# Rotary attention: row maxima of short key spans taken for two or four heads in one instruction, in 38 pieces over 19 of 20 steps

## The chip, the cores and the metric

One core of one Trainium2 chip runs the whole layer in one launch. The metric is the device time of that launch in microseconds, median of several runs.

## The reference

A layer of four residual parts on x of 1024 tokens and 512 channels. Only the first is touched:

```python
x = x + attn_a(layernorm(x))     # rotary, 32 heads of 16: the part changed
x = x + ffn(layernorm(x)); x = x + attn_b(layernorm(x)); x = x + ffn(layernorm(x))
# attn_a, causal, T = 1024:
scores = einsum('bqhd,bkhd->bhqk', rot(xq), rot(xk)) * 16 ** -0.5   # masked where k > q
out = einsum('bhqk,bkhd->bqhd', softmax(scores), xv).reshape(B, T, C) @ wo.T
```

## The kernel before

Rotary attention works on 8 groups of GA = 4 heads. To keep the softmax exact, the maximum of every row of scores must be known before the exponentials. So each group is scored twice. The first scoring, with queries on the partitions, exists only for the maxima: TensorE (PE) writes a *piece*, a 128-query tile against up to 512 keys, into one bank of PSUM (L940, and a causal mask added by a second matmul, L943, where the piece touches the diagonal), and VectorE (DVE) reduces it to one number per row (L1041). A group has 48 pieces, for each head 8 query tiles, of 128, 256, 384 or 512 keys, tiles 4 to 7 with a second span. The maxima of the 4 x 8 units are then split into three bf16 parts (`split_max`, five short DVE instructions in a chain, L552 to L561), turned by PE (`turn_max`, L949), copied out (L1046) and stored by three DMAs as three extra rows of the queries. The second scoring (L968, mask L972) contracts over 99 rows, so that the maximum comes off in the matmul itself; ScalarE (ACT) takes the exponential of two banks at once (L1028, L1030); PE multiplies by the values (`mix`, L986, fp32, four heads in strips of 32 columns).

The order is written by hand. Each group has 20 steps. In step `tau`, PE does the second scoring of one set of heads, then the `mix` blocks that are due, then the pieces of the *next* group that `a_pieces_before` gives to step t' = (tau + 6) mod 20 (A_SHIFT = 6), and, where due, `turn_max` and the turning of the output rows (L995). DVE follows the same list: maxima of the pieces, `split_max` at t' = SPLIT_AT, copy of the turned maxima at t' = MAX_AT. `a_pieces_before` deals the pieces out in equal shares of width + 128 over the first A_LAST_PIECE steps t'. Below, "step n" is step n of the group that is being exponentiated, so t' = 0 is step 14, t' = 17, 18, 19 are steps 11, 12, 13. `mix` blocks fall into steps 0, 1, 5, 6, 7, 11, 12, 15, 16 and 19; the output rows are turned in steps 2 and 8.

The pieces have three banks (4, 5, 7): PE must wait for the maximum of the piece three before. The engines are in order, so a PE wait for a bank also holds the next scoring, and with it ACT. The second scoring of a step waits for the exponential of two steps before.

`FirstMaxima` does the pieces of group 0, with six banks, between the projections of the values (L499, L502, reduce L538), and then as many pieces of group 1 as t' = 0 to 5 hold (`score_next`, L515, L518, reduce L546), before the loop of the 8 groups starts. After the loop comes `stream_block`, everything from the output projection of this attention on.

Of the kernel before, what the change touches and what calls it, by code (L numbers as in the profile page):

```python
# [11 lines left out]
ALU = mybir.AluOpType  # L12
ACT = mybir.ActivationFunctionType
AX = mybir.AxisListType

P = 128
T = 1024
C = 512
NT = T // P
KC = C // P  # L20
W = 512
# [3 lines left out]
GA = 4  # L25
# [15 lines left out]
def key_spans(i):  # L41

    w = P * (i + 1)
    return [(0, min(w, W))] + ([(W, w)] if w > W else [])
# [370 lines left out]
A_ROWS = 6 * DA  # L415
A_UNITS = GA * NT
A_LINKS = 5
A_TERMS = ((0, 0), (0, 1), (0, 2), (1, 0), (1, 1), (2, 0))
A_PIECES = [(hh, i, c, span) for hh in range(GA) for i in range(NT) for c, span in enumerate(key_spans(i))]
A_FIRST = sorted(A_PIECES, key=lambda piece: piece[1])  # L420
A_LAST_PIECE = 17
A_SHIFT = 6
A_PIECE_BANKS = (4, 5, 7)


def a_pieces_before(t):

    total = sum(k1 - k0 + W // 4 for _, _, _, (k0, k1) in A_PIECES)
    n, width = 0, 0
    while n < len(A_PIECES) and width * A_LAST_PIECE < t * total:  # L430
        width += A_PIECES[n][3][1] - A_PIECES[n][3][0] + W // 4
        n += 1
    return n


class FirstMaxima:
# [52 lines left out]
    def score_pieces(self, pe, h):  # L489
        pe.wait_ge(self.made, 2)  # L490
        pe.wait_ge(self.rows_in[h], 16 * 2 * len(A_TERMS))
        for n, (hh, i, c, (k0, k1)) in enumerate(A_FIRST):
            if i // 2 != h:
                continue
            if n >= len(self.BANKS):
                pe.wait_ge(self.credited["piece_max"], 1 + n + 1 - len(self.BANKS))
            out = self.ps[:, self.BANKS[n % len(self.BANKS)], 0:k1 - k0]
            last_span = k1 == P * (i + 1)
            last = pe.matmul(out, self.q_st[0][0:A_ROWS, hh, i * P:(i + 1) * P], self.k_st[0][0:A_ROWS, hh, k0:k1],  # L499
                             start=True, stop=not last_span)  # L500
            if last_span:
                last = pe.matmul(out[:, k1 - k0 - P:k1 - k0], self.const["ident_bf"][:, :], self.mask[:, :],  # L502
                                 start=False, stop=True)
            last.then_inc(self.credited["piece_scored"], 1)

    def score_next(self, pe, first, end):

        for n in range(first, end):
            hh, i, c, (k0, k1) = A_PIECES[n]
            if n == 0:  # L510
                pe.wait_ge(self.loaded[1], 16 * 2 * len(A_TERMS))
            pe.wait_ge(self.credited["piece_max"], 1 + len(A_PIECES) + n + 1 - len(A_PIECE_BANKS))
            out = self.ps[:, A_PIECE_BANKS[n % len(A_PIECE_BANKS)], 0:k1 - k0]
            last_span = k1 == P * (i + 1)
            last = pe.matmul(out, self.q_st[1][0:A_ROWS, hh, i * P:(i + 1) * P], self.k_st[1][0:A_ROWS, hh, k0:k1],  # L515
                             start=True, stop=not last_span)
            if last_span:
                last = pe.matmul(out[:, k1 - k0 - P:k1 - k0], self.const["ident_bf"][:, :], self.mask[:, :],  # L518
                                 start=False, stop=True)
            last.then_inc(self.credited["piece_scored"], 1)  # L520

    def turn_max(self, pe):
# [9 lines left out]
        dve.wait_ge(self.made, 2)  # L532

    def max_of_pieces(self, dve):
        for n, (hh, i, c, (k0, k1)) in enumerate(A_FIRST):
            u = hh * NT + i
            dve.wait_ge(self.credited["piece_scored"], 1 + n + 1)
            dve.tensor_reduce(self.part_max[:, c, u:u + 1], self.ps[:, self.BANKS[n % len(self.BANKS)], 0:k1 - k0],  # L538
                              AX.X, ALU.max).then_inc(self.credited["piece_max"], 1)

    def max_of_next(self, dve, first, end):
        for n in range(first, end):
            hh, i, c, (k0, k1) = A_PIECES[n]
            u = hh * NT + i
            dve.wait_ge(self.credited["piece_scored"], 1 + len(A_PIECES) + n + 1)
            dve.tensor_reduce(self.part_max[:, c, u:u + 1], self.ps[:, A_PIECE_BANKS[n % len(A_PIECE_BANKS)], 0:k1 - k0],  # L546
                              AX.X, ALU.max).then_inc(self.credited["piece_max"], 1)

    def split_max(self, dve, start=1, pieces_done=None):
        link = self.credited["link"]  # L550
        dve.wait_ge(self.credited["piece_max"], 1 + len(A_FIRST) if pieces_done is None else pieces_done)
        dve.tensor_tensor(self.row_max[:, :], self.part_max[:, 0, :], self.part_max[:, 1, :], ALU.max).then_inc(link, 1)  # L552
        dve.wait_ge(link, start + 1)
        dve.tensor_scalar(self.max_part[:, 0, :], self.row_max[:, :], -1.0, None, ALU.mult).then_inc(link, 1)
        dve.wait_ge(link, start + 2)
        dve.scalar_tensor_tensor(self.max_rest[:, :], self.row_max[:, :], -1.0, self.max_part[:, 0, :],
                                 ALU.mult, ALU.subtract).then_inc(link, 1)
        dve.wait_ge(link, start + 3)
        dve.tensor_copy(self.max_part[:, 1, :], self.max_rest[:, :]).then_inc(link, 1)
        dve.wait_ge(link, start + 4)  # L560
        dve.tensor_tensor(self.max_part[:, 2, :], self.max_rest[:, :], self.max_part[:, 1, :],  # L561
                          ALU.subtract).then_inc(link, 1)
# [7 lines left out]
def rotary_projection_block(nc, ctx, norm, weights, xt_h, xt_l, w_h, w_l, v_all, o_all, spare, stage_room, first, const, ps, parts_dram, x_in):  # L570
# [4 lines left out]
    with ExitStack() as own:  # L575
# [65 lines left out]
        def _(pe):  # L641
# [53 lines left out]
            first.score_next(pe, 0, 2)  # L695
            first.turn_max(pe)
            first.score_next(pe, 2, a_pieces_before(A_SHIFT))

        @block.scalar
# [42 lines left out]
        def _(dve):  # L742
# [32 lines left out]
            first.max_of_next(dve, 0, 2)  # L775
            first.take_max(dve)
            first.max_of_next(dve, 2, a_pieces_before(A_SHIFT))


# [14 lines left out]
def rotary_attention_block(nc, ctx, v_all, o_all, spare, wo_h, wo_l, first, const, ps, parts_dram, wo_dram, raw_room, later_loads):  # L794
# [9 lines left out]
    def sem(name):  # L804
        return credited[name] if name in credited else ctx.enter_context(nc.semaphore(f"ra_{name}"))
# [3 lines left out]
    UNITS = A_UNITS  # L809
    PIECES = A_PIECES  # L810
    NP = len(PIECES)
    SPLIT_AT, MAX_AT = 17, 18
    ROWS = A_ROWS + A_PARTS
    LINKS = A_LINKS
    PIECE_BANKS = A_PIECE_BANKS
    SHIFT = A_SHIFT
    with ExitStack() as own:
        def sb(name, shape, dt=F32):
            return own.enter_context(nc.sbuf_tensor(f"ra_{name}", shape, dt))

        q_st = first.q_st + [sb(f"q_st{b}", [P, GA, T], BF16) for b in range(2, A_BUFS)]
        k_st = first.k_st + [sb(f"k_st{b}", [P, GA, T], BF16) for b in range(2, A_BUFS)]
        v4 = [sb(f"v4{b}", [P, NT, GA, 32]) for b in range(2)]
        pt = [sb("pt0", [P, GA, 2 * W]), sb("pt1", [P, GA, 2 * W]), spare.rearrange("p (h n) -> p h n", h=GA)]
        mask, part_max, max_part, max_rows = first.mask, first.part_max, first.max_part, first.max_rows
# [9 lines left out]
        piece_max = sem("piece_max")  # L835
# [15 lines left out]
        def loads_of(g):  # L851

            return g // A_BUFS + 1 - (1 if g % A_BUFS == 0 else 0)

        def count(each, g, n):
            return 1 + each * g + n
# [70 lines left out]
        @block.tensor  # L927
        def _(pe):
            def piece(g, n):

                hh, i, c, (k0, k1) = PIECES[n]
                b = g % A_BUFS
                if n == 0:
                    pe.wait_ge(loaded[b], 16 * 12 * loads_of(g))
                pe.wait_ge(piece_max, count(NP, g, n + 1 - len(PIECE_BANKS)))
                if n == 0:
                    pe.wait_ge(max_out, count(1, g, 0))
                out = ps[:, PIECE_BANKS[n % len(PIECE_BANKS)], 0:k1 - k0]
                last_span = k1 == P * (i + 1)
                last = pe.matmul(out, q_st[b][0:A_ROWS, hh, i * P:(i + 1) * P], k_st[b][0:A_ROWS, hh, k0:k1],  # L940
                                 start=True, stop=not last_span)
                if last_span:
                    last = pe.matmul(out[:, k1 - k0 - P:k1 - k0], const["ident_bf"][:, :], mask[:, :],  # L943
                                     start=False, stop=True)
                last.then_inc(piece_scored, 1)

            def turn_max(g):
# [51 lines left out]
            for tau in range(NGA * S + 3):  # L999
# [3 lines left out]
                for gg in range(NGA):  # L1003
                    for k in range(SETS):
                        n = tau - (S * gg + A_SET_END[k] + 2)
# [29 lines left out]
        @block.vector  # L1035
        def _(dve):
            def max_of_piece(g, n):
                hh, i, c, (k0, k1) = PIECES[n]
                u = hh * NT + i
                dve.wait_ge(piece_scored, count(NP, g, n + 1))  # L1040
                dve.tensor_reduce(part_max[:, c, u:u + 1], ps[:, PIECE_BANKS[n % len(PIECE_BANKS)], 0:k1 - k0], AX.X, ALU.max).then_inc(piece_max, 1)  # L1041

            def take_max(g):
                dve.wait_ge(max_turned, count(1, g, 1))
# [1007 lines left out]
```

## Time and profile before

| | us |
|---|---|
| runs | 1602.8, 1601.39, 1602.74; median 1602.74 |
| profiled execution | 1604.81, span of its instructions 1603.0 |
| rotary attention loop in it | 140.3 to about 404 |
| TensorE busy | 1507.2 (94%) |
| VectorE busy | 1111.8 (69%) |
| ScalarE busy | 796.5 (50%) |
| mean granted TensorE clock | 0.984 |

Busy time counts an instruction from its start to its last result; on PE and DVE the next one starts before that, so shares of busy time overstate how full an engine is. The granted clock is 1.00 at 2.4 GHz and 0.50 at 1.2 GHz.

### The profile page before, as it was taken

What the parts mean: (1) busy time and instruction counts of PE and PEld (TensorE: products, weight loads), DVE (VectorE), ACT (ScalarE), POOL (GpSimd) and SP (SyncE); (2) the same over time, 40 slices, a digit from 0 to 9 for tenths busy, and PEclk for the clock granted to TensorE, in tenths of its full rate; (3) what the DMA queues carried; (4) which work ended last, traced back from release to release, by engine and by line L of the source; (5) the groups of instructions that cost most, each with busy time, mean ns of one, the idle gap of its engine ahead of it and who ended that gap; (6) DMA issues with size and microseconds to landing.
All of it is one profiled execution on the core that took longest, in us unless ns stands there. A gap on an engine that the chain in (4) does not pass through costs nothing.

```text
span 1603.0 us, 25452 instructions
## 1 busy us (share of the span) xinstructions
PE 1507.2 (94%) x8968; PEld 1174.6 (73%) x8968; DVE 1111.8 (69%) x2866; ACT 796.5 (50%) x2087; POOL 440.3 (27%) x435
## 2 busy tenths in 40 slices
PE   3998999998897899999999999999999999999997
PEld 2863444443686788888888888888888888888776
DVE  5658777771575577687678677678767767767873
ACT  3522555557333355555555555555554555555441
POOL 4102000010452341341332234144134143224332
PEclk9997999999999899999999999999999999999999
DMA  4363344301100100100100010010010010000000
GB/s 150 96 140 56 41 61 59 43 2 54 54 21 1 40 27 1 40 21 8 40 14 14 1 40 27 1 40 27 1 40 27 1 40 14 14 19 22 7 21 27
DMA packets 40206, 54.27 MB, mean 34 GB/s; under 512 B 5776, under 2 KB 21392, under 8 KB 40080
## 3 DMA queue, kind: packets, MB, share of 16 engines
q1 hardware_dynamic: 40080, 52.65, 13.8%
q8 instruction: 72, 1.18, 0.3%
q14 instruction: 54, 0.44, 0.1%
HBM read 44.04 MB, written 8.39 MB: 33 GB/s over the span
## 4 chain that ended last, share of the span: by engine, by line
PE 65%; DVE 3%; issue 2%; POOL 2%; ACT 2%; POOLq 0%; ACTq 0%; DVEq 0%
PE ps L50 18%; PE ps L52 18%; PE ps L51 18%; PE ps L1528 7%; PE ps L1503 2%; DVE ab_qt_l L1777 1%; POOL ab_o_l L1424 1%; PE ps L241 1%; PE ps L1505 0%; ACT ab_o_raw L1695 0%; POOL wo L1392 0%; ACT ab_kt_h L1674 0%; POOL ab_o_h L1422 0%; DVE ab_pt_l L1785 0%; ACT ab_squares L1665 0%
## 5 line engine op out<-in xcount | busy, mean ns | idle before, releaser
L1653 ACT ACTIVATE prob<-prob,ab_neg_max 128x128 f32<-128x128 f32 (+7 forms) x256 | 200.7, 784 | 241.7 <-DVE ab_neg_max L1768 240.6
L1785 DVE TENSOR_TENSOR ab_pt_l<-ps,ab_pt_h 128x512 fp32r<-128x512 f32 x288 | 198.0, 688 | 67.3 <-ACT ab_pt_h L1681 65.0
L1681 ACT CAST ab_pt_h<-ps 128x512 fp32r<-128x512 f32 x288 | 171.7, 596 | 127.2 <-PE ps L1528 126.6
L1768 DVE CUSTOM_DVE_ANT_0 prob<-ps,rel 128x512 f32<-128x512 f32 (+3 forms) x256 | 146.1, 571 | 102.6 <-PE ps L52 101.8
L50 PE MATMUL ps<-ab_w_h,ab_xt_h 128*128 128x512 f32 (+1 forms) x512 | 185.6, 362 | 5.0 <-DVE ab_v_l L1805 5.0
L1041 DVE TENSOR_REDUCE ra_part_max<-ps 128x1 f32<-128x512 f32 (+3 forms) x318 | 156.4, 552 | 48.3 <-PE ps L943 29.2
L1528 PE MATMUL ps<-ident,prob 128*128 128x128 f32 x1152 | 173.4, 273 | 4.6 <-DVE ab_qt_l L1777 3.3
L52 PE MATMUL ps<-ab_w_h,ab_xt_l 128*128 128x512 f32 (+1 forms) x512 | 174.4, 341 | 0.0
L51 PE MATMUL ps<-ab_w_l,ab_xt_h 128*128 128x512 f32 (+1 forms) x512 | 173.7, 339 | 0.0
L1793 DVE TENSOR_SCALAR prob<-prob,ab_recip 128x128 f32<-128x128 f32 (+7 forms) x256 | 164.1, 641 | 9.1
L1413 POOL TENSOR_TENSOR ab_rms<-ab_ms_eps,neg_half 128x5 f32<-128x5 f32 x64 | 76.3, 1192 | 318.0 <-DVE ab_ms_eps L1810 317.2
L1528 PEld LDWEIGHTS ps<-ident,prob 128*128 128x128 f32 x1152 | 138.1, 140 | 24.8 <-DVE ab_qt_l L1777 4.3
L1030 ACT ACTIVATE ra_pt<-ps 128x1024 f32<-128x1024 f32 x96 | 97.3, 1024 | 84.9 <-PE ps L972 72.7
L50 PE MATMUL ps<-ab_kt_h,ab_qt_h 128*128 128x512 f32 (+2 forms) x384 | 132.8, 346 | 0.2 <-DVE ab_neg_max L1768 0.2
L52 PE MATMUL ps<-ab_kt_h,ab_qt_l 128*128 128x512 f32 (+2 forms) x384 | 132.1, 344 | 0.0
L51 PE MATMUL ps<-ab_kt_l,ab_qt_h 128*128 128x512 f32 (+2 forms) x384 | 131.8, 343 | 0.0
L50 PE MATMUL ps<-ab_pt_h,ab_v_h 128*128 128x512 f32 x288 | 127.2, 442 | 2.5 <-ACT ab_o_raw L1695 2.3
L1422 POOL CAST ab_o_h<-ab_o_raw 128x512 fp32r<-128x512 f32 x64 | 42.0, 657 | 289.0 <-ACT ab_o_raw L1695 257.1
L51 PE MATMUL ps<-ab_pt_l,ab_v_h 128*128 128x512 f32 x288 | 113.6, 394 | 0.0
L52 PE MATMUL ps<-ab_pt_h,ab_v_l 128*128 128x512 f32 x288 | 113.6, 394 | 0.0
L50 PEld LDWEIGHTS ps<-ab_w_h,ab_xt_h 128*128 128x128 f32 x512 | 97.8, 191 | 19.6 <-DVE ab_v_l L1805 5.9
L51 PEld LDWEIGHTS ps<-ab_w_l,ab_xt_h 128*128 128x128 f32 x512 | 98.0, 191 | 14.1
(232 smaller groups left out, 3487.9 us busy)
## 6 DMA issues: line engine op xcount, KB each, us to landing
f_raw<-in_wqkv SPq DMA_DIRECT2D x32, 384.0 KB, 3.7
f_raw<-in_wbo SPq DMA_DIRECT2D x32, 256.0 KB, 2.6
ra_first_rows<-parts SPq DMA_DIRECT2D x36, 128.0 KB, 6.7
parts<-pa_stage SPq DMA_DIRECT2D x12, 256.0 KB, 3.1
parts<-f_raw SPq DMA_DIRECT2D x12, 256.0 KB, 3.3
ra_q_st<-parts SPq DMA_DIRECT2D x24, 128.0 KB, 6.5
ra_k_st<-parts SPq DMA_DIRECT2D x24, 128.0 KB, 6.8
f_raw<-in_wf SPq DMA_DIRECT2D x8, 324.0 KB, 3.3
```

Source lines behind the costliest of these rows:

```text
L50: pe.matmul(out, lh, rh, start=start, stop=False)
L51: pe.matmul(out, lh, rl, start=False, stop=False)
L52: return pe.matmul(out, ll, rh, start=False, stop=stop)
L1030: act.activation(pt[k % 3][:, h, :], pair.rearrange("p a b -> p (a b)"), ACT.Exp).then_inc(exped, 1)
L1041: dve.tensor_reduce(part_max[:, c, u:u + 1], ps[:, PIECE_BANKS[n % len(PIECE_BANKS)], 0:k1 - k0], AX.X, ALU.max).then_inc(piece_max, 1)
L1413: pool.tensor_tensor(rms[:, t % 2, :], ms_eps[:, t % 2, :], const["neg_half"][:, 0:GB + 1], ALU.pow).then_inc(rms_ready, 1)
L1528: last = pe.transpose(ring_bank("p", u, j)[:, h * P:(h + 1) * P], prob[:, u % 2, h, j * P:(j + 1) * P], const["ident"][:, :])
L1653: act.activation(prob[:, t % 2, h, 0:w], prob[:, t % 2, h, 0:w], ACT.Exp, bias=neg_max[:, t % 2, h, pieces_per_head(t % NT) - 1:pieces_per ...
L1681: act.copy(pt_h[:, n % PT, :], ring_bank("p", u, j)).then_inc(pt_high, 1)
L1768: dve.tensor_tensor_reduce(out=prob[:, t % 2, h, k0:k1], in0=ps[:, n % 2, a:b], in1=const["rel"][:, SLIDE - i * P + k0:SLIDE - i * P + k1] ...
L1785: dve.tensor_tensor(pt_l[:, n % PT, :], ring_bank("p", u, j), pt_h[:, n % PT, :].bitcast(F32), ALU.subtract).then_inc(emptied, 1)
L1793: dve.tensor_scalar(prob[:, t % 2, h, 0:w], prob[:, t % 2, h, 0:w], recip[:, t % 2, h:h + 1], None, ALU.mult).then_inc(normed, 1)
```

## The change

Spans of 128 keys are scored for four heads and spans of 256 for two heads into one bank, one head behind the other, and one `tensor_reduce` with a three-dimensional operand takes the maxima of all of them. Spans of 384 and 512 keys stay as they are. A group has 38 pieces in place of 48, ordered by query tile instead of by head, in the loop as well. Every matmul stays. A_LAST_PIECE goes from 17 to 19, SPLIT_AT from 17 to 18 and MAX_AT from 18 to 19. The diff, cut to its core (the three places that score and the three that reduce all call the new functions):

```diff
-A_PIECES = [(hh, i, c, span) for hh in range(GA) for i in range(NT) for c, span in enumerate(key_spans(i))]
-A_FIRST = sorted(A_PIECES, key=lambda piece: piece[1])
-A_LAST_PIECE = 17
+def a_pieces():
+    pieces = []
+    for i in range(NT):
+        for c, (k0, k1) in enumerate(key_spans(i)):
+            heads = min(GA, W // (k1 - k0))
+            pieces += [(hh, heads, i, c, (k0, k1)) for hh in range(0, GA, heads)]
+    return pieces
+A_PIECES = a_pieces()
+A_LAST_PIECE = 19
 def a_pieces_before(t):
-    total = sum(k1 - k0 + W // 4 for _, _, _, (k0, k1) in A_PIECES)
+    total = sum(heads * (k1 - k0) + W // 4 for _, heads, _, _, (k0, k1) in A_PIECES)
     n, width = 0, 0
     while n < len(A_PIECES) and width * A_LAST_PIECE < t * total:
-        width += A_PIECES[n][3][1] - A_PIECES[n][3][0] + W // 4
+        _, heads, _, _, (k0, k1) = A_PIECES[n]
+        width += heads * (k1 - k0) + W // 4
         n += 1
     return n
+def score_piece_a(pe, piece, bank, q_rows, k_rows, ident, mask):
+    first, heads, i, _, (k0, k1) = piece
+    for hh in range(first, first + heads):
+        out = bank[:, (hh - first) * (k1 - k0):(hh - first + 1) * (k1 - k0)]
+        last_span = k1 == P * (i + 1)
+        last = pe.matmul(out, q_rows[0:A_ROWS, hh, i * P:(i + 1) * P], k_rows[0:A_ROWS, hh, k0:k1],
+                         start=True, stop=not last_span)
+        if last_span:
+            last = pe.matmul(out[:, k1 - k0 - P:k1 - k0], ident[:, :], mask[:, :], start=False, stop=True)
+    return last
+def max_of_piece_a(dve, part_max, piece, bank):
+    first, heads, i, c, (k0, k1) = piece
+    maxima = part_max[:, c, :].rearrange("p (h i) -> p h i", i=NT)
+    return dve.tensor_reduce(maxima[:, first:first + heads, i],
+                             bank[:, 0:heads * (k1 - k0)].rearrange("p (h k) -> p h k", h=heads), AX.X, ALU.max)
...
-    SPLIT_AT, MAX_AT = 17, 18
+    SPLIT_AT, MAX_AT = 18, 19
```

## Rows read from the trace of the kernel before

**Rows 1.** The page, part 1 (busy us) and the granted clock of part 2.
```profile
PE 1507.2 (94%) x8968; PEld 1174.6 (73%) x8968; DVE 1111.8 (69%) x2866; ACT 796.5 (50%) x2087; POOL 440.3 (27%) x435
...
PEclk9997999999999899999999999999999999999999
```
**Rows 2.** Busy time by stretch (windows): group 3, and group 7, which has no pieces.
```profile
243.70:277.70 34.00, 32.36 (x270) 14.82 (x273) 25.81 (x59) 19.51 (x22) 0.61 (x1) 1.00 0.38 47
...
376.70:400.00 23.30, 20.23 (x175) 7.89 (x178) 1.36 (x4) 18.45 (x21) 1.27 (x1) 1.00 0.21 69
```
**Rows 3.** The turning of the maxima, source view of L949: first and last start.
```profile
L949 PE MATMUL ps<-ident_bf,ra_max_part x7: 257/257/257, 163.3 to 367.4; 128*96 128x128 bf16 x7
```
**Rows 4.** Groups by form, 0 to 330 us, two forms of L1041; then timeline, DVE.
```profile
L1041 DVE TENSOR_REDUCE ra_part_max<-ps 128x1 f32<-128x512 f32 x134 | 89.2, 684 | 25.8 <-PE ps L940 16.3 <-PE ps L943 9.5
...
L1041 DVE TENSOR_REDUCE ra_part_max<-ps 128x1 f32<-128x128 f32 x44 | 12.4, 282 | 4.7 <-PE ps L943 4.7
...
257.84 2.55 DVE L1041 TENSOR_REDUCE ra_part_max<-ps 128x1 f32<-128x384 f32 x5 [0.61 <-PE ps L943]
```
**Rows 5.** Timeline, PE matmuls, steps 6 to 8 of group 3: start, duration.
```profile
255.93 0.27 PE L940 MATMUL ps<-ra_first_rows 96*128 96x256 bf16 x1
256.04 0.22 PE L943 MATMUL ps<-ra_mask,ident_bf 128*128 128x128 bf16 x1
256.10 0.59 PE L968 MATMUL ps<-ra_q_st,ra_k_st 99*128 99x512 bf16 x2
256.62 0.86 PE L986 MATMUL ps<-ra_pt,ra_v 128*32 128x128 f32 x16
257.41 0.34 PE L940 MATMUL ps<-ra_first_rows 96*128 96x384 bf16 x1
...
258.14 0.60 PE L968 MATMUL ps<-ra_q_st,ra_k_st 99*128 99x512 bf16 x2
258.57 0.22 PE L940 MATMUL ps<-ra_first_rows 96*128 96x128 bf16 x1
```
**Rows 6.** Waits in group 3, 243.7 to 277.7: total us, times, longest.
```profile
PEld ps L940 <- DVE ra_part_max L1041: 10.0, 20, 0.8
...
DVE ra_part_max L1041 <- PE ps L943: 4.4, 7, 1.2
```
**Rows 7.** Timeline, ACT: step 2 to 3 of group 3, and of group 7.
```profile
247.80 1.02 ACT L1030 ACTIVATE ra_pt<-ps 128x1024 f32<-128x1024 f32 x1 [0.45 <-PE ps L972]
250.31 1.02 ACT L1030 ACTIVATE ra_pt<-ps 128x1024 f32<-128x1024 f32 x1 [1.49 <-PE ps L972]
...
379.77 1.02 ACT L1030 ACTIVATE ra_pt<-ps 128x1024 f32<-128x1024 f32 x1
381.12 1.02 ACT L1030 ACTIVATE ra_pt<-ps 128x1024 f32<-128x1024 f32 x1 [0.33 <-PE ps L972]
```
**Rows 8.** Timeline around the turning of the maxima in group 2.
```profile
229.63 0.19 DVE L552 TENSOR_TENSOR ra_row_max<-ra_part_max 128x32 f32<-128x32 f32 x1
...
230.52 0.19 DVE L561 TENSOR_TENSOR ra_max_part<-ra_max_rest,ra_max_part 128x32 bf16<-128x32 f32 x1
...
231.34 0.12 PEld L949 LDWEIGHTS ps<-ident_bf,ra_max_part 128*96 128x96 bf16 x1 [0.84 <-DVE ra_max_part L561]
```
**Rows 9.** Timeline ahead of the loop, DVE and PE.
```profile
110.31 6.99 DVE L538 TENSOR_REDUCE ra_part_max<-ps 128x1 f32<-128x512 f32 x16 [3.25 <-PE ps L499]
...
137.78 2.02 DVE L546 TENSOR_REDUCE ra_part_max<-ps 128x1 f32<-128x384 f32 x4 [0.17 <-PE ps L518]
...
114.72 0.48 PE L50 MATMUL ps<-a_w_h,wo 128*128 128x512 f32 x1
...
131.06 0.34 PE L524 MATMUL ps<-ident_bf,ra_max_part 128*96 128x128 bf16 x1 [1.21 <-DVE ra_max_part L561]
```
**Rows 10.** Windows of PE at a low share, with the granted clock.
```profile
84.00:88.00 4.00, 1.43 (x11) 1.13 (x10) 2.37 (x6) 2.61 (x7) 0.00 (x0) 1.00 0.88 269
88.00:92.00 4.00, 4.00 (x13) 3.12 (x12) 1.78 (x3) 1.14 (x2) 0.00 (x0) 0.57 0.17 49
...
1500.00:1505.00 5.00, 3.31 (x26) 2.96 (x24) 3.64 (x9) 2.98 (x8) 0.00 (x0) 1.00 0.00 0
```

More of the change, by code:

```diff
@@ L491, in score_pieces @@
         pe.wait_ge(self.rows_in[h], 16 * 2 * len(A_TERMS))
-        for n, (hh, i, c, (k0, k1)) in enumerate(A_FIRST):
-            if i // 2 != h:
+        for n, piece in enumerate(A_PIECES):
+            if piece[2] // 2 != h:
                 continue
@@ L496, in score_pieces @@
                 pe.wait_ge(self.credited["piece_max"], 1 + n + 1 - len(self.BANKS))
[L497 to L503, printed above, removed]
+            last = score_piece_a(pe, piece, self.ps[:, self.BANKS[n % len(self.BANKS)], :], self.q_st[0], self.k_st[0],
+                                 self.const["ident_bf"], self.mask)
             last.then_inc(self.credited["piece_scored"], 1)
@@ L508, in score_next @@
         for n in range(first, end):
-            hh, i, c, (k0, k1) = A_PIECES[n]
             if n == 0:
@@ L512, in score_next @@
             pe.wait_ge(self.credited["piece_max"], 1 + len(A_PIECES) + n + 1 - len(A_PIECE_BANKS))
[L513 to L519, printed above, removed]
+            last = score_piece_a(pe, A_PIECES[n], self.ps[:, A_PIECE_BANKS[n % len(A_PIECE_BANKS)], :], self.q_st[1],
+                                 self.k_st[1], self.const["ident_bf"], self.mask)
             last.then_inc(self.credited["piece_scored"], 1)
@@ L534, in max_of_pieces @@
     def max_of_pieces(self, dve):
-        for n, (hh, i, c, (k0, k1)) in enumerate(A_FIRST):
-            u = hh * NT + i
+        for n, piece in enumerate(A_PIECES):
             dve.wait_ge(self.credited["piece_scored"], 1 + n + 1)
-            dve.tensor_reduce(self.part_max[:, c, u:u + 1], self.ps[:, self.BANKS[n % len(self.BANKS)], 0:k1 - k0],
-                              AX.X, ALU.max).then_inc(self.credited["piece_max"], 1)
+            max_of_piece_a(dve, self.part_max, piece, self.ps[:, self.BANKS[n % len(self.BANKS)], :]
+                           ).then_inc(self.credited["piece_max"], 1)
     def max_of_next(self, dve, first, end):
         for n in range(first, end):
-            hh, i, c, (k0, k1) = A_PIECES[n]
-            u = hh * NT + i
             dve.wait_ge(self.credited["piece_scored"], 1 + len(A_PIECES) + n + 1)
-            dve.tensor_reduce(self.part_max[:, c, u:u + 1], self.ps[:, A_PIECE_BANKS[n % len(A_PIECE_BANKS)], 0:k1 - k0],
-                              AX.X, ALU.max).then_inc(self.credited["piece_max"], 1)
+            max_of_piece_a(dve, self.part_max, A_PIECES[n], self.ps[:, A_PIECE_BANKS[n % len(A_PIECE_BANKS)], :]
+                           ).then_inc(self.credited["piece_max"], 1)
     def split_max(self, dve, start=1, pieces_done=None):
         link = self.credited["link"]
-        dve.wait_ge(self.credited["piece_max"], 1 + len(A_FIRST) if pieces_done is None else pieces_done)
+        dve.wait_ge(self.credited["piece_max"], 1 + len(A_PIECES) if pieces_done is None else pieces_done)
         dve.tensor_tensor(self.row_max[:, :], self.part_max[:, 0, :], self.part_max[:, 1, :], ALU.max).then_inc(link, 1)
@@ L929, in piece @@
             def piece(g, n):
-                hh, i, c, (k0, k1) = PIECES[n]
                 b = g % A_BUFS
@@ L937, in piece @@
                     pe.wait_ge(max_out, count(1, g, 0))
[L938 to L944, printed above, removed]
+                last = score_piece_a(pe, PIECES[n], ps[:, PIECE_BANKS[n % len(PIECE_BANKS)], :], q_st[b], k_st[b],
+                                     const["ident_bf"], mask)
                 last.then_inc(piece_scored, 1)
@@ L1037, in max_of_piece @@
             def max_of_piece(g, n):
-                hh, i, c, (k0, k1) = PIECES[n]
-                u = hh * NT + i
                 dve.wait_ge(piece_scored, count(NP, g, n + 1))
-                dve.tensor_reduce(part_max[:, c, u:u + 1], ps[:, PIECE_BANKS[n % len(PIECE_BANKS)], 0:k1 - k0], AX.X, ALU.max).then_inc(piece_max, 1)
+                max_of_piece_a(dve, part_max, PIECES[n], ps[:, PIECE_BANKS[n % len(PIECE_BANKS)], :]).then_inc(piece_max, 1)
             def take_max(g):
```

## The prediction

> **What bounds the kernel now.** I read the page first: PE is busy 94% of the span at almost full clock, DVE 69% [rows 1]. That is an average over stages, so I cut out the stage that changes. The maxima are turned once per group, 7 times between 163.3 and 367.4, so a group takes (367.4 - 163.3) / 6 = 34.0 us [rows 3]. In a group PE is busy 32.4 us, DVE 25.8, ACT 19.5 [rows 2]. These figures count instructions that overlap, so what an engine really needs must come from start to start.
>
> PE [rows 5]: a matmul of 256 columns 0.11 us (255.93 to 256.04), one of 128 0.06, two of 512 0.43 (258.14 to 258.57), so 0.215 each and 0.16 for 384; `mix` blocks of 256 and 128 columns together 0.79 (256.62 to 257.41), about 1.05 for 512. Each of the two scorings has 8 matmuls of 128, 8 of 256, 8 of 384, 24 of 512 and 32 masks: 0.48 + 0.88 + 1.28 + 5.16 + 1.92 = 9.7 us. The `mix` has 4608 columns, 9 x 1.05 = 9.5 us. With about 1 us for turning rows and maxima: 19.4 + 9.5 + 1 = 29.9 us. The group takes 34.0, so PE stands still for about **4.1 us** of it.
>
> DVE [rows 4]: a reduce of 512 shows 684 ns, one of 128 shows 282. But five in a row (384, 512, 512, 128, 512, whose durations add to 2.88 with 0.555 for 384 between its neighbours) take 2.55 us, so each next one starts 0.083 before the end of the last. Start to start it is 0.60 for 512, 0.465 for 384, 0.33 for 256, 0.20 for 128: 0.13 per 128 columns and about 0.065 per instruction. The 48 reduces need 8 x (0.20 + 0.33 + 0.465) + 24 x 0.60 = 22.4 us, all DVE work about 25 of 34. DVE isn't the bound on average.
>
> What the two do to each other is the loss. The view of waits shows PE's weight loads of pieces waiting for DVE 20 times, 10.0 us (part of it under matmuls still running), and DVE waiting for PE 7 times, 4.4 us, in the same group [rows 6]. The two alternate, because three banks hold only three pieces. In step 2, where four pieces fall, ACT's rhythm is 2.51 us against 1.35 in group 7 without pieces [rows 7]. The four pieces and their masks need 0.79 on PE; the other 0.4 is waiting.
>
> **The change, part by part.** *Matmuls*: none is removed; PE's 29.9 us stay. *Reduces*: 8 of 128 become 2 of 4 x 128, 8 of 256 become 4 of 2 x 256. At the price of a plain 512 they take 6 x 0.60 against 8 x 0.20 + 8 x 0.33, 3.6 against 4.25: DVE saves **0.65 us** per group. The trace has no reduce of several rows. Bounds: the cost of one plain 512 (0.60) from below; from above four separate 128s (0.80) and two 256s (0.66), 0.65 dearer per group in all, which is the old cost. I take 0.60, since start to start goes with the columns. DVE has slack, so of this nothing counts directly; the rest is in how the pieces fall.
>
> The Trainium skill ("VectorE: DVE Perf Modes", "The DRAIN you can't avoid") says that the next DVE instruction doesn't start until the pipe is empty, so each reduce would hold DVE for all of its shown duration. By that the ten instructions fewer would save 10 x 0.148 = 1.5 us per group. The trace doesn't agree: 2.88 us of durations fit in 2.55.
>
> *Spreading*: 48 pieces in 17 steps put 2 to 4 pieces, 0.8 to 1.6 us of DVE, into a step; the dearest bursts lie in steps without `mix` (2, 4, 10, 14, 17, 18), where PE itself needs only 1.0 to 1.2 us, so it runs into the banks. 38 in 19 put 1 to 3, nearly always 2 (1.2 us), into a step. I carried three clocks (PE, DVE, ACT) through the 20 steps with the durations above and ACT's 1.02 (0.60 for the short sets), once for each dealing, every instruction starting when its engine is free and what it waits for is done. Waits for a bank, before: steps 2, 4, 8, 10, 14, 18 with 0.7, 0.7, 0.4, 0.6, 0.2, 0.9, and 0.1 elsewhere, **3.6 us**. After: steps 8, 10, 18 with 0.2, 0.6, 0.1, **0.9 us**, and 0.1 for an exponential. The walk over the old pieces gives a group of 33.1 us, 0.9 short of the 34.0 measured, so I trust its difference more than its level.
>
> *SPLIT and MAX one step later*: this is a wait that is added. Before, the last pieces fall in step 10, `split_max` follows in step 11, and PE asks for it in step 12, after two scorings and two `mix` blocks of 512, over 2.5 us of other work. The chain L552 to L561 takes 230.52 + 0.19 - 229.63 = 1.08 us, and was done at 230.71 while PE came to L949 at 231.34: no wait [rows 8]; the 0.84 shown there is under a running `mix`. After, the last piece is in step 12 and `turn_max` in step 13, which has no `mix`: between them PE has one scoring, 0.43 to 0.54 us. DVE needs the last pieces (0.6 to 1.0 us with latency), then the chain 1.1, then about 0.1. PE waits 0.6 + 0.6 + 1.1 + 0.1 - 0.5, in the walk **1.7 us**, in every one of the 7 groups. Queued behind it on PE is the scoring of step 14, for which ACT then waits; on DVE the copy of the turned maxima. Bounds: 1.2 if DVE is level with PE, 2.9 if it is two pieces behind. Nothing covers it. The stores of the maxima are then issued a step later but still 6 steps, some 10 us, ahead of their use in step 0, and the queue of SP has nothing behind them for the next 3 us; I cost them at nothing. The first piece of the next group waits for the copy of the turned maxima (0.4 us), under the scoring of step 14.
>
> Per group: 3.6 - 0.9 - 0.1 - 1.7 = **0.9 us**, 6 times; the last group with pieces gets only steps 0 to 13 of it, 0.6. Loop: 6 x 0.93 + 0.6 = 6.2 us.
>
> *Ahead of the loop*: DVE sets the pace there. In the stretch of tiles 4 and 5, 16 reduces take 6.99 us, and PE is let on to the projections at 114.72 [rows 9], when the tenth of 16 is reduced (110.31 + 5 x 0.60 + 4 x 0.20 + 0.33 = 114.4). With 11 pieces it is the fifth: 110.31 + 5 x 0.60 + 0.1 = 113.4, and PE is through 0.34 later, at 113.8: 0.9 us earlier, and all behind it too. The tail, from the turning at 131.06 to the end of the last reduce, 137.78 + 2.02 = 139.80 [rows 9], holds 18 reduces, 9.5 us by duration and 8.0 start to start; with 13 (9 x 0.60 + 4 x 0.465) it holds 7.3, and with the waits for PE that it has now the gain is 0.6 to 0.9 us. Together **1.8 us**. Clock is low there (slices 3 and 4 of the row [rows 1]), but DVE leads.
>
> *After the loop* nothing changes, and its start waits for the end of the loop, not for a load.
>
> Sum: 6.2 + 1.8 = 8.0 us. The profiled execution, 1604.81, would be 1596.8; it lies 2.07 above the median, so the median goes to 1602.74 - 8.0 = **1594.7 us**.
>
> **Rivals.** (a) *The new wait takes the gain.* If DVE comes to step 12 two pieces behind, PE waits 2.9 us, not 1.7, and the group gains 3.5 - 0.9 - 2.9 = -0.3 to 0; what is left is the 1.8 us ahead of the loop: 1600.9. Against: steps 11 and 12 have a `mix` of 512 each, in which DVE catches up. For: they now hold pieces, which before they didn't.
>
> (b) *More is gained.* If the banks hardly ever fill, the 0.9 that I leave goes too, and the wait at the turning is 1.2: 0.9 + 0.9 + 0.5 = 2.3 per group, but part of it meets ACT's 1.02 per step in the light steps; with 1.6 per group, 6.6 x 1.6 + 1.8 = 12.4: 1590.3.
>
> (c) *Slower: the clock.* A stand of 1.7 us in each group might let the granted clock fall. After a stretch with PE busy 1.43 of 4 us it fell, to a mean of 0.57 over the next 4 [rows 10]; at 1.2 GHz for 3.4 us (0.43 x 4 / 0.5) PE loses half of them, 1.7 us. Seven times is 12 us, more than the 8.0: 1606.7. It decides as soon as it happens in 5 of 7 groups. Against: 1500 to 1505 has PE busy 3.31 of 5, the same 1.7 us standing, and the clock stays at 1.00. The Trainium skill has the rule ("TensorE: Matmul & The Clock Gate", "HAM oscillation — how this bites in real kernels"): idling between bursts of matmuls brings the clock down and costs more than the idling. By it alone this rival would be the likelier one; the row of 1500 speaks against it at this size.
>
> (d) *Merged reduces cost as their parts.* Then DVE loses its 0.65 us; a third of it at most comes through at full banks: 1.5 us less gain, 1596.2. This is inside the forecast's range.
>
> **How the numbers follow.** Forecast 0.66, with (d) in it, spread 1591.5 to 1598; (b) 0.15, (a) 0.13, (c) 0.06. The range for 8 in 10 goes from 1590 to 1600.9, into (b) and up to (a). A measurement of this kernel tells about 0.2%, 3.2 us, from no change, so faster is the forecast and (b), 0.81; same is (a), 0.13; slower is (c), 0.06.
>
> **What would show it.** Right: period of L949 about 33.1 us; PE's waits for L1041 fewer than half; a wait of PE for L561 of 1.5 to 2 us uncovered, once per group; reduces of 4 x 128 at about 684 ns; the loop's first scoring at about 138.5 instead of 140.3; the clock 1.00 from 146 to the end of the loop. Wrong: a period of 34 with the wait at L561 near 3 us is (a), a clock of 0.50 behind the turnings is (c), a period below 32.5 is (b). If the period stays and the wait is as forecast, the walk's account of the bank waits was wrong.

## The result, and the profile after

The changed kernel takes 1592.18 us (median of 4 runs, 1591.04 to 1593.13) against 1602.77 (1601.39 to 1602.94): ratio 0.9936, 95% interval 0.9918 to 0.9953, faster by 10.6 us. Forecast were 1594.7 in 1590 to 1600.9. The profiled execution took 1592.62. One of the four runs of the kernel over 17 steps, below, took 2144.83 us at a mean granted clock of 0.655 and is left out of its median.

The page of the changed kernel, busy time and granted clock, answers [rows 1]:

```profile
PE 1493.7 (94%) x8968; PEld 1170.9 (74%) x8968; DVE 1106.1 (70%) x2786; ACT 795.9 (50%) x2087; POOL 440.7 (28%) x435
...
PEclk9997999999999999999999999999999999999999
```

PE has the same 8968 matmuls, DVE 80 instructions fewer (8 groups of ten). The shares are the same as before; they don't tell that anything has happened. Where the time went is read from the places that can be matched in both traces. First the turning of the maxima (L960 now, L949 in [rows 3]), in the source view:

```profile
L960 PE MATMUL ps<-ident_bf,ra_max_part x7: 257/257/257, 160.3 to 359.1; 128*96 128x128 bf16 x7
```

(359.1 - 160.3) / 6 = **33.13 us** per group, against 34.0. Then the first exponential of group 0 and of group 7, timeline of ACT, before and after:

```profile
141.63 1.02 ACT L1030 ACTIVATE ra_pt<-ps 128x1024 f32<-128x1024 f32 x1 [20.50 <-PE ps L972]
...
376.76 1.02 ACT L1030 ACTIVATE ra_pt<-ps 128x1024 f32<-128x1024 f32 x1 [1.12 <-PE ps L972]
```

```profile
139.03 1.02 ACT L1041 ACTIVATE ra_pt<-ps 128x1024 f32<-128x1024 f32 x1 [19.09 <-PE ps L983]
...
367.44 1.02 ACT L1041 ACTIVATE ra_pt<-ps 128x1024 f32<-128x1024 f32 x1 [1.12 <-PE ps L983]
```

| part of the span | before | after | difference |
|---|---|---|---|
| ahead of the loop, to the first exponential | 141.6 | 139.0 | -2.6 |
| groups 0 to 6 | 235.1 | 228.4 | -6.7 |
| group 7 and all behind it | 1226.2 | 1223.1 | -3.1 |
| span | 1603.0 | 1590.5 | -12.5 |

The last part of the span, with 3.1 us of difference, has no changed instruction in it. Windows of the 200 us from the start of group 7, before and after (the columns are as in [rows 2]; the third from the end is the granted clock):

```profile
376.80:576.80 200.00, 175.93 (x1021) 137.94 (x1015) 110.24 (x323) 84.15 (x229) 68.17 (x85) 0.94 0.10 31
```

```profile
367.50:567.50 200.00, 174.60 (x1036) 137.20 (x1029) 111.54 (x327) 85.38 (x232) 71.60 (x89) 0.97 0.10 31
```

The clock is 0.94 before and 0.97 after: some 12 us less at 1.2 GHz fit in (0.03 x 200 / 0.5), and 15 matmuls more have started. Over the whole part the clock record has 26.5 us at 1.2 GHz before and 15.3 after. The twelve kernels of this case don't differ here, and in their traces the two go together: from 15 us at 1.2 GHz and 1223.1 us for this part to 26.5 us and 1226.3 us. So these 3.1 us are put down to the clock, not to the change.

Below, a *stand* is time in which PE could run nothing. The new one, in the timeline of group 3 (start, duration, idle before in brackets):

```profile
257.36 0.39 PE L454 MATMUL ps<-ra_first_rows 96*128 96x512 bf16 x1
...
257.65 0.59 PE L979 MATMUL ps<-ra_q_st,ra_k_st 99*128 99x512 bf16 x2
257.85 0.69 DVE L464 TENSOR_REDUCE ra_part_max<-ps 128x1 f32<-128x512 f32 x1 [0.80 <-PE ps L457]
...
258.57 0.19 DVE L570 TENSOR_TENSOR ra_row_max<-ra_part_max 128x32 f32<-128x32 f32 x1
...
259.46 0.19 DVE L579 TENSOR_TENSOR ra_max_part<-ra_max_rest,ra_max_part 128x32 bf16<-128x32 f32 x1
259.70 0.26 PE L960 MATMUL ps<-ident_bf,ra_max_part 128*96 128x128 bf16 x1 [1.46 <-DVE ra_max_part L579]
...
260.61 1.02 ACT L1041 ACTIVATE ra_pt<-ps 128x1024 f32<-128x1024 f32 x1 [1.31 <-PE ps L983]
```

The last piece of the group is issued at 257.36. DVE waits 0.80 for it, so it has no older piece left to do. It reduces this one and runs its chain. PE, which had one scoring to do, stands 1.46 us with nothing running, and ACT then waits 1.31 for the next scoring. In [rows 8] the same wait was drawn as 0.84 under a running `mix` and cost nothing. And waits of PE between 140 and 400, before and after:

```profile
PE ps L940 <- DVE ra_part_max L1041: 9.9, 40, 0.5
```

```profile
PE ps L960 <- DVE ra_max_part L579: 10.2, 7, 1.5
...
PE ps L454 <- DVE ra_part_max L464: 2.8, 7, 0.4
```

The 9.9 us in 40 waits for the reduces are now 2.8 in 7, but 10.2 for the chain come in. Taken as they are, these rows say that PE waits *more* than before, although the loop is shorter. The view begins a wait only at the modelled end of the matmul in front, and so leaves part of each stand out. An example from before, in step 2 of group 3:

```profile
248.30 0.22 PE L943 MATMUL ps<-ra_mask,ident_bf 128*128 128x128 bf16 x1
248.82 0.34 PE L940 MATMUL ps<-ra_first_rows 96*128 96x384 bf16 x1 [0.30 <-DVE ra_part_max L1041]
```

From start to start these are 0.52 us, the mask takes 0.06 of them, and 0.46 are a stand; the bracket says 0.30. Counted in this way for one group with the clock at 1.00 (what a start lies behind the one before it, less that matmul's columns at 2.4 GHz, stretches of over 0.03 us, the starts of and behind `mix` blocks left out; the last four kernels are experiments, below):

| kernel | period, us | stands at the banks | stand before the turning | period less all stands |
|---|---|---|---|---|
| before | 34.0 | 3.3 | 0 | 30.7 |
| changed | 33.1 | 0.8 | 1.6 | 30.7 |
| merged, 17 steps | 32.4 | 1.7 | 0 | 30.7 |
| merged, 18 steps | 32.5 | 1.4 | 0.4 | 30.7 |
| order alone, 17 steps | 33.4 | 2.7 | 0 | 30.7 |
| spreading alone (group with the clock at 1.00) | 35.5 | 2.8 | 1.9 | 30.7 |

The last column is the same for all within 0.1, so these two kinds of stand are the whole difference between the kernels' periods. The change takes away 2.5 us per group at the banks and adds 1.6 before the turning. The merged reduces cost what a plain one costs (groups by form, 0 to 330):

```profile
L464 DVE TENSOR_REDUCE ra_part_max<-ps 128x1 f32<-128x512 f32 x168 | 106.6, 684 | 27.4 <-PE ps L454 18.8 <-PE ps L457 8.1
...
L464 DVE TENSOR_REDUCE ra_part_max<-ps 128x2 f32<-128x512 f32 x30 | 19.9, 685 | 6.6 <-PE ps L457 6.6
L464 DVE TENSOR_REDUCE ra_part_max<-ps 128x4 f32<-128x512 f32 x15 | 10.4, 692 | 11.2 <-PE ps L457 11.2
```

### The profile page after: what moved, and what is told of

The parts are those of the page before. It is cut to its first block, busy times and chain, and to the rows that moved or that the text cites. A ratio compares the mean times of both kernels' runs of the same rounds, so it can differ in the third digit from the quotient of the medians.

```text
span 1590.5 us, 25372 instructions
## 1 busy us (share of the span) xinstructions
PE 1493.7 (94%) x8968; PEld 1170.9 (74%) x8968; DVE 1106.1 (70%) x2786; ACT 795.9 (50%) x2087; POOL 440.7 (28%) x435
## 4 chain that ended last, share of the span: by engine, by line
PE 65%; DVE 3%; issue 2%; POOL 2%; ACT 2%; POOLq 0%; ACTq 0%; DVEq 0%
PE ps L50 18%; PE ps L52 18%; PE ps L51 18%; PE ps L1537 7%; PE ps L1512 2%; DVE ab_qt_l L1786 1%; POOL ab_o_l L1433 1%; PE ps L241 1%; PE ps L1514 0%; ACT ab_o_raw L1704 0%; POOL wo L1401 0%; ACT ab_kt_h L1683 0%; POOL ab_o_h L1431 0%; DVE ab_pt_l L1794 0%; ACT ab_squares L1674 0%
## 5 line engine op out<-in xcount | busy, mean ns | idle before, releaser
L464 DVE TENSOR_REDUCE ra_part_max<-ps 128x1 f32<-128x512 f32 (+3 forms) x304 | 182.2, 656 | 62.0 <-PE ps L457 40.7
L1041 ACT ACTIVATE ra_pt<-ps 128x1024 f32<-128x1024 f32 x96 | 97.9, 1024 | 91.0 <-PE ps L983 74.1
```

The costliest lines, as they stand in the source:

```text
L464: return dve.tensor_reduce(maxima[:, first:first + heads, i], bank[:, 0:heads * (k1 - k0)].rearrange("p (h k) -> p h k", h=heads), AX.X, A ...
L1041: act.activation(pt[k % 3][:, h, :], pair.rearrange("p a b -> p (a b)"), ACT.Exp).then_inc(exped, 1)
```

## The experiments

Theory A is the prediction's: time was lost where DVE fills the three banks; the change takes most of that away and pays for the later turning. The change does three things at once (merging, a new order, 19 steps for 17), so the first four runs take them apart. The measure is the *period*, the time from one turning of the maxima to the next, taken from the first and the last of the seven. It repeats within 0.02 us from group to group as long as the clock stays the same, and doesn't see the clock behind the loop.

**Merged pieces over 17 steps, split and turning where they were.**

```diff
-A_LAST_PIECE = 19
+A_LAST_PIECE = 17
-    SPLIT_AT, MAX_AT = 18, 19
+    SPLIT_AT, MAX_AT = 17, 18
```

> Merged pieces, but dealt over 17 steps with the split and the turning where they were before the change (17, 18). Theory A (the gain comes from full banks that don't fill any more, and the later turning costs a wait of 1.5 us per group): the wait of PE before the turning goes, some bank waits come back; period of a group 33.14 - 0.8 = 32.3 us, total about 1587, faster than the changed kernel by some 5 us. Rival B (the gain is the spreading over 19 steps): most of the gain goes, period near 34, total above 1598.

```profile
L960 PE MATMUL ps<-ident_bf,ra_max_part x7: 257/257/257, 159.4 to 353.6; 128*96 128x128 bf16 x7
```

Period (353.6 - 159.4) / 6 = 32.37 us, forecast 32.3; 1589.8 us (three runs), ratio to before 0.9912 (0.9892 to 0.9932), forecast 1587. Rival B falls: the step from 17 to 19 doesn't bring the gain, it costs 0.77 us per group. PE's waits show the trade:

```profile
PE ps L454 <- DVE ra_part_max L464: 5.6, 14, 0.5
```

PE's waits for banks double from 2.8 to 5.6 us in the loop, and the 10.2 for the chain are gone from the view. From start to start it is the same: 0.9 us more per group at the banks, 1.6 less before the turning.

**Merged over 18 steps.** A_LAST_PIECE = 18, the rest as in the changed kernel.

> As the changed kernel, but the pieces are dealt over 18 steps; split and turning stay at 18 and 19. Theory A: the last pieces are done a step before the turning, PE waits for it 0.4 to 0.6 us instead of 1.5; bank waits up by 0.5; period 33.14 - 0.55 = 32.6 us, total about 1588.5. Rival B: between the changed kernel and the one over 17, that is a little slower than the changed one.

Period (352.6 - 157.6) / 6 = 32.50 us, forecast 32.6; 1588.46 us, ratio 0.9907 (0.989 to 0.9923). One step between the last piece and the turning is enough to bring the wait down: the view has 1.7 us in 7 waits in all. The total is below the one over 17 steps although the period is longer. In the profiled executions that is the stretch ahead of the loop, which this one left 2.7 us earlier, at a clock of 0.76 between 120 and 140 against 0.65. The two totals can't be told apart.

**The spreading alone**: the kernel before with A_LAST_PIECE = 19 and SPLIT_AT, MAX_AT = 18, 19.

> The kernel before with its 48 pieces in their old order, dealt over 19 steps, split and turning at 18 and 19. Theory A: bank waits hardly fall (one piece per bank is still a short reduce followed by long ones), the wait before the turning comes, about 2 us; period 34.0 + 1.4 = 35.4 us, total about 1612, slower than before. Rival B: most of the change's gain, period 33 to 33.5, total about 1596.

1619.49 us, ratio 1.0097 (1.008 to 1.0114): 16 us *slower* than before, and 7 more than A had said. The waits have the form that A gave, here of PE between 140 and 400:

```profile
PE ps L949 <- DVE ra_max_part L561: 12.5, 7, 1.8
PE ps L940 <- DVE ra_part_max L1041: 9.2, 27, 0.6
```

But the period, (385.7 - 165.5) / 6 = 36.7 by the source view, is 1.3 above the forecast. The turnings lie 35.46 us apart once, behind the one of group 3, and 36.9 to 37.0 us the other five times. Windows behind a turning, in group 2 (turned at 239.32) and in group 3 (at 276.35):

```profile
241.00:244.40 3.40, 3.40 (x17) 0.92 (x16) 1.02 (x2) 1.27 (x2) 0.00 (x0) 0.51 0.50 96
278.00:281.40 3.40, 3.40 (x33) 1.37 (x31) 1.94 (x4) 1.83 (x3) 0.00 (x0) 1.00 0.19 51
```

After the stand that ends at 239 the granted clock is 0.51 for 3.4 us, and the window has 17 matmuls; after the equal one that ends at 276 it stays 1.00, and the window has 33. So in this kernel the prediction's rival (c) happened, five times, at 1.4 to 1.6 us each (it had said 1.7). Where it didn't, A's period holds, 35.46 against 35.4. A's reason holds too: by the table above the stands at the banks fall only from 3.3 to 2.8.

**The order alone**: no merging, but pieces by query tile; 17 steps.

```diff
-            heads = min(GA, W // (k1 - k0))
+            heads = 1
```

> 48 pieces, none merged, but ordered by query tile instead of by head; 17 steps, split 17, turning 18. Tells the merging from the new order, both of which the change makes. Theory A: the order alone gives part, by the three clocks 0.6 us per group (period 33.4), total about 1598. Rival C (what counts is ten reduces and ten waits fewer): nothing, period 34.0.

1599.35 us (10 runs), ratio 0.9976 (0.9966 to 0.9985); period (363.0 - 162.7) / 6 = 33.38, forecast 33.4. It has ten reduces per group more than the changed kernel, and yet it gains 0.6 us per group on the kernel before. By head, short and long pieces alternate; by tile, like stands with like, and the steps get other bursts. Step 2 holds two pieces in place of four, and its stand goes from 0.66 us to none; step 18 goes from 0.88 to 0.43; the other steps together have 0.5 more. Why this order suits the steps better than another wasn't tested. Rival C falls as the whole story. Merging on top of it (32.37) gives another 1.0.

**Does the number of reduces count?** The changed kernel, banks shared, but one reduce for each head.

```diff
-    return dve.tensor_reduce(maxima[:, first:first + heads, i],
-                             bank[:, 0:heads * (k1 - k0)].rearrange("p (h k) -> p h k", h=heads), AX.X, ALU.max)
+    n = k1 - k0
+    for hh in range(heads):
+        u = (first + hh) * NT + i
+        last = dve.tensor_reduce(part_max[:, c, u:u + 1], bank[:, hh * n:(hh + 1) * n], AX.X, ALU.max)
+    return last
```

> The changed kernel, pieces still share banks, but the maxima of a bank are taken by one reduce for each head (four of 128, two of 256), 10 reduces more in a group. Theory A: DVE gives back its 0.65 us, of which 0.1 to 0.2 comes through at full banks: period 33.3 us. Rival (fewer DVE instructions are the gain): period 33.8 or more.

Period (359.2 - 159.7) / 6 = 33.25, 0.11 longer; 1594.89 us in one run. Ten DVE instructions fewer per group are worth 0.1 us of period. So of the 1.0 that merging brings, 0.9 must come from the banks: one bank carries four heads, or two, ten handovers between PE and DVE fewer per group, and with them another dealing of the pieces to the steps. These last two weren't taken apart.

**Is the wait before the turning on the path in full?** The last link of the chain is done again, two and four times more.

```diff
-A_LINKS = 5
+A_LINKS = 7
...
+        for extra in range(2):
+            dve.wait_ge(link, start + 5 + extra)
+            dve.tensor_tensor(self.max_part[:, 2, :], self.max_rest[:, :], self.max_part[:, 1, :],
+                              ALU.subtract).then_inc(link, 1)
```

> The changed kernel with the last instruction of the chain that splits the maxima done three times (7 links, not 5; same result), so that PE waits 0.44 us longer before the turning, 1.9 to 2.0 us. Theory A: the wait lies on the path in full: period 33.14 + 0.44 = 33.6 us. Theory C (the clock falls when PE stands for about 1.8 us in a group, as in the kernel with the spreading alone, where it was low for 20 us of the loop): some groups a further 1.5 us longer, at a granted clock of 0.5 for 3.4 us each.

> As before with 9 links, 0.88 us more, PE stands 2.4 us before the turning. Theory A: period 34.0 us, loop 6 us longer than in the changed kernel. Theory C: the clock falls in most groups, period 35.5, loop 14 to 16 us longer.

The waits of PE before the turning, in the kernel with two links more, and with four:

```profile
PE ps L964 <- DVE ra_max_part L583: 13.4, 7, 1.9
```

```profile
PE ps L964 <- DVE ra_max_part L583: 16.5, 7, 2.4
```

With two more, three of the six periods last 33.59 or 33.60 (0.45 longer, A) and three 35.19 or 35.20. The one run took 1603.06 us, and the kernel before, run beside it, 1603.52: nearly all of the gain is gone. With four more, all six periods are 34.05, (368.1 - 163.8) / 6, 0.91 longer, A again. The clock keeps its 1.00 behind the first six stands, though they are longer, and falls once, at the last turning, for 6.9 us at 0.51. The one run took 1606.53 us, and its loop is 10.4 us longer than in the changed kernel, not 6: 4.5 of it in groups 1 to 5, the rest in group 0, which begins with 5 us at half clock against 2.6, and in group 6 with its fall. So the wait counts in full, and theory C is half right: a stand of 1.8 to 1.9 us *can* be followed by a fall of the clock, a longer one needn't. Windows with two links more, behind the turning of group 0 (at 161.13) and of group 2 (at 231.52):

```profile
162.30:165.70 3.40, 3.40 (x21) 1.38 (x18) 1.33 (x2) 1.78 (x2) 0.00 (x0) 0.50 0.29 73
232.70:236.10 3.40, 3.40 (x34) 1.89 (x32) 2.09 (x4) 1.78 (x2) 0.00 (x0) 1.00 0.31 72
```

The stand in front is 1.9 us both times, so its length alone doesn't decide; what does is left open. In the changed kernel, with 1.5 us, the clock fell in no group.

**Ahead of the loop**: the changed kernel with the 48 single pieces for group 0 (`FirstMaxima` alone; the counts of the loop are shifted by ten).

> The changed kernel in the loop, but the 48 unmerged pieces for the first group, ahead of the loop. Theory A: the projections behind tiles 4 and 5 start 0.9 us later relative to the start of their pieces, period as in the changed kernel (33.14), the loop starts 0.9 to 1.2 us later than in the changed kernel. Rival (the 2.6 us that the start of the loop came earlier are the clock's): no difference beyond where the clock is low.

The stretch of tiles 4 and 5, the DVE timeline of the changed kernel, and then of this one:

```profile
110.08 6.68 DVE L464 TENSOR_REDUCE ra_part_max<-ps 128x1 f32<-128x512 f32 x11 [3.25 <-PE ps L454]
...
119.59 9.13 DVE L464 TENSOR_REDUCE ra_part_max<-ps 128x1 f32<-128x512 f32 x16 [2.83 <-PE ps L454]
```

```profile
110.71 6.99 DVE L467 TENSOR_REDUCE ra_part_max<-ps 128x1 f32<-128x512 f32 x16 [3.25 <-PE ps L457]
...
121.19 9.13 DVE L467 TENSOR_REDUCE ra_part_max<-ps 128x1 f32<-128x512 f32 x16 [3.48 <-PE ps L457]
```

From the first burst to the next are 9.51 us with merged pieces and 10.48 with single ones (10.47 in the kernel before), 0.97 apart, at a clock of 1.00 in both. The period is (360.5 - 161.6) / 6 = 33.15; one run, 1594.61 us. That the loop starts 1.04 later (first exponential at 140.07 against 139.03) looks like the same number, but two things cancel in it: this execution came to the stretch 0.63 later (110.71 against 110.08), and behind the last reduce ahead of the loop, where its clock was back at 1.00 and the other's at 0.50, it was 0.55 faster. So 1.0 of the 2.6 us is settled by the burst alone. 0.2 was there already when the stretch began (110.08 against 110.31 in [rows 9]); the other 1.4 is the tail with 13 pieces in place of 18, which this kernel keeps (7.4 us in both), so it is read from the traces only.

**Two versions meant to be better**: A_SHIFT = 7, all pieces a step earlier, so that two `mix` blocks lie in front of the turning again; over 17 steps with 17, 19, and over 18 with 18, 19.

> A version meant to beat both: merged pieces over 17 steps, everything of the next group a step earlier (A_SHIFT 7, so the steps without pieces are 10 to 12), split at 17, turning at 19, which is step 12 as before the change, where two blocks of the mix lie between. Theory A: no wait for the chain, period 32.37 - 0.2 = 32.15 us, loop 222 us, total about 1588, within noise of the kernels over 17 and 18 steps. If period stays above 32.4, the three clocks don't tell 0.2 us apart.

> Merged pieces over 18 steps, A_SHIFT 7, split 18, turning 19 (step 12). Theory A: the wait for the chain lies under the mix of step 12's predecessor, period 32.5 us, total about 1588.5, the same as over 18 steps with shift 6.

Periods (352.5 - 159.6) / 6 = 32.15 and (354.7 - 159.7) / 6 = 32.50, as forecast. Totals 1588.88 us, ratio 0.9913 (0.9899 to 0.9926), and 1591.38, ratio 0.9928 (0.9913 to 0.9944), the second 2.9 above its forecast. The first has the shortest loop of all, 221.2 us against 223.3 over 17 steps with A_SHIFT = 6. But a part of that is only moved: with A_SHIFT = 7 two pieces more are done ahead of the loop, which starts 1.0 later. Its total isn't lower than the others' over 17 or 18 steps, because the 1.1 us left are less than what the clock does outside the loop. All four versions with 17 or 18 steps lie below the changed kernel, by 0.8 to 3.7 us; the intervals of their ratios to before overlap with its own, so by the totals no best one can be named, by the period it is 17 steps with A_SHIFT 7.

## Why the prediction was right

- *PE's 29.9 us of 34.0, DVE not the bound*: held in the main; period less stands is 30.7 in all kernels. Reducing DVE's work alone (the experiment on the number of reduces, turned round) moves the period by 0.1; changing only the order or the dealing moves it by 0.6 to 1.5. The 0.8 that PE's sum lacks is one term: ahead of each of the ten `mix` blocks the start comes 0.095 us later than the columns in front take, 0.95 per group in every kernel, and the sum had nothing for it. So the walk was 0.9 short in both kernels.
- *A reduce of several rows at the price of a plain one*: 685 and 692 ns against 684. Right; rival (d) is out. The rule of the Trainium skill that the prediction sets against the trace ("VectorE: DVE Perf Modes", "The DRAIN you can't avoid") has an exception in its own section: an instruction that isn't held starts earlier. So reduces that start 0.083 us before the end of the last one don't contradict the section.
- *Bank waits 3.6 to 0.9, new wait 1.7, net 0.9 per group*: the period fell by 0.87, and the terms hold one by one. Start to start, the stands at the banks are 3.3 before and 0.8 after, the one before the turning 1.6. By steps, before: 2, 4, 8, 10, 14 and 18 have 0.66, 0.66, 0.37, 0.59, 0.16 and 0.88 (forecast 0.7, 0.7, 0.4, 0.6, 0.2, 0.9). After: 8 and 10 have 0.18 and 0.57 (0.2, 0.6). So the 0.87 isn't luck. ACT shows it as well: step 2, with 2.51 and 1.35 us in [rows 7], is now 1.49. One reason given was wrong: the dearest bursts don't all lie in steps without `mix`; steps 5 and 7 have a `mix` and three pieces of 384, 512 and 512 keys, and PE doesn't stand there.
- *Parts of the new wait*: from the last piece written to its maximum DVE took 0.9 us, not 0.6 + 0.6, since the last step holds one piece and DVE had none left over; chain 1.1 and one scoring of 0.43 as forecast. But the bound of 1.2 for DVE without arrears was too low: this is that case, and PE stood 1.6.
- *The sign that I named for it*: I wrote that PE's waits for the maxima would be fewer than half. In PE's own row they are (9.9 in 40 to 2.8 in 7). In the row of its weight loads, on which the argument rested [rows 6], they went only from 10.0 in 20 to 8.8 in 14 (group 3 of the changed kernel, below). Against stands of 3.3 and 0.8 us both figures are mostly waits under running matmuls, as in [rows 8]; that row was a poor witness.

```profile
PEld ps L454 <- DVE ra_part_max L464: 8.8, 14, 0.9
```

- *Loop 6.2*: 6.7 measured. Groups 1 to 5 give 0.87 each, group 6 0.55, group 0 1.86. Group 0 begins at half clock in both traces, in the changed kernel for 2.6 us of it and before for 4.7; the last microsecond is put down to that, not shown.
- *Ahead of the loop 1.8*: 2.6. Its first term, 0.9, is right (0.97). The mis-sized term is the tail, forecast 0.6 to 0.9. Measured: before, from the end of the chain's last link (131.0) to 139.80, 8.8 us; after, 129.8 to 137.2, 7.4, so 1.4. I had charged the new tail with the same waits of DVE for PE as the old; the trace has the last 11 reduces running in one piece:

```profile
131.07 6.12 DVE L464 TENSOR_REDUCE ra_part_max<-ps 128x2 f32<-128x512 f32 x11
```

- *After the loop nothing*: no work changed, but the profiled executions differ by 3.1 us there through the clock. The medians, 10.6 apart, hold less of it than the profiles, 12.2 apart. What the profiles show of the change itself is the 9.3 us in front of group 7, less about 1.2 that are put down to the clock of group 0 and to the earlier start of the stretch: 8.1, against 8.0 forecast. The medians, with the clock in them, lie 10.6 apart, and it is a matter of luck how near that comes to the sum.
- *Rival (c), slower by the clock, 0.06*: it didn't happen in this kernel, but the mechanism is real, and near. Two instructions of 0.22 us more in the chain, and three of seven groups pay 1.6 us. The argument against it, the window at 1500 with the same 1.7 us standing and full clock, was true and weak: one place where it doesn't fall doesn't say that it can't. It deserved more than 0.06. The Trainium skill's rule ("TensorE: Matmul & The Clock Gate", "HAM oscillation — how this bites in real kernels"), that idling between bursts costs clock as well, agrees with the kernel with two links more (0.50 behind three of seven stands) and not with the first six stands of the one with four. The case in that section has waits of 3 to 5 us between bursts, longer than any stand here, so by itself it didn't make this rival the likelier one.
- What the prediction didn't ask: whether the third part of the change belongs to the other two. Its own numbers held it: 2.7 us of bank waits gone (2.5 measured), 1.7 paid (1.6) for a step too few behind the last piece. Over 17 steps the period is 0.77 shorter still.

## What to carry to other kernels

Where two in-order engines share a few banks, count how bursts fall into steps, not only sums: here neither engine was full, order alone gave 0.6 us of 34, and sharing banks, with the dealing that goes with it, another 1.0. Measure such stands from start to start; a view that begins at the end of the instruction in front can leave half of them out. When work is spread over more steps, look at what must follow its last item: here a chain of 1.1 us needed a step with other work between, or the next engine stood for it in full. And keep stands of the matmul engine short: one of 1.9 us cost its own length in one group, and nearly twice that in the next, where the clock fell behind it.

## What was not expected of the hardware

The granted clock fell behind stands of PE of 1.8 and 1.9 us in a loop that is otherwise dense (five of seven and three of seven groups), and not behind the first six stands of 2.4 us in another kernel, nor behind those of 1.5 us in the changed one (all groups). Each of these eight falls took 3.4 us at 1.2 GHz and cost 1.4 to 1.6 us. Stands of one length in one kernel had both outcomes, so the length alone doesn't decide; what does isn't settled by these runs. The kernels with two and with four links more were run once each.

A reduce that delivers four maxima per row from one bank takes 692 ns, one that delivers a single one from the same 512 columns 684.
